# Inverse square roots of a two-layer graph network: from eight VectorE steps to one power on GpSimd

## The reference, cut to what matters

```python
x = _layernorm(x + _L0_gnn_ref(x, ...))   # attention over edges and self loops, then elu, residual, norm
x = _layernorm(x + _L1_gnn_ref(src, dst, x, edge_attr_3, ...))
...
# in _L0_gnn_ref
h = x + jax.nn.elu(proj)
out = (h - mu) * jax.lax.rsqrt(var + LN_EPS) * gamma + beta
...
# in _L1_gnn_ref
d = jax.nn.gelu(layer_norm(x @ Wd1 + bd1, g1, b1), approximate=False)
d = jax.nn.gelu(layer_norm(d @ Wd2 + bd2, g2, b2), approximate=False)
logits = w1[target] - w2[source] + d
out = jax.ops.segment_sum(a * (w3[source] + d), target, num_segments=m)   # a: softmax over a target's edges
```

## Time and profile before

| | us |
|---|---|
| runs, median of 3 | 2307.57 |
| runs, lowest and highest | 2290.02, 2311.89 |
| span of the profiled execution | 2281.3 |
| TensorE busy | 1697.7 (74%) |
| VectorE busy | 1608.6 (71%) |
| GpSimd busy | 1071.7 (47%) |
| ScalarE busy | 704.6 (31%) |

### The profile page before, as it was taken

One profiled execution on the slowest core, in us unless ns is written; L12 is line 12 of the kernel. 1 busy time (PEld: TensorE's weight loads), 2 busy tenths in 40 slices (PEclk: granted clock), 3 DMA queues, 4 the chain that ended last, 5 costly groups with the idle time before them and its releaser, 6 DMA issues. The chain is left out here.

```text
span 2281.3 us, 29583 instructions
## 1 busy us (share of the span) xinstructions
PE 1697.7 (74%) x6749; PEld 925.5 (41%) x6749; DVE 1608.6 (71%) x4249; ACT 704.6 (31%) x1168; POOL 1071.7 (47%) x1254
## 2 busy tenths in 40 slices
PE   6888798888878880099999999358676766667673
PEld 4555565555555540023333333247433333333331
DVE  2667676676767678657666766448598887878786
ACT  2545454454555440012222222025311111111111
POOL 3555554455555440002434444610267676667764
PEclk9999898999999985579778988668799888889886
DMA  2333333343334341101111111100112111112120
GB/s 69 102 110 123 108 120 109 103 125 108 120 113 126 107 115 35 27 11 25 37 33 36 39 35 31 35 5 3 30 43 47 42 46 41 46 44 50 43 49 14
DMA packets 154993, 142.83 MB, mean 63 GB/s; under 512 B 83688, under 2 KB 103103, under 8 KB 154948
## 3 DMA queue, kind: packets, MB, share of 16 engines
q1 hardware_dynamic: 122948, 112.22, 16.2%
q0 software_dynamic: 32000, 30.10, 6.7%
HBM read 71.30 MB, written 73.65 MB: 64 GB/s over the span
## 5 line engine op out<-in xcount | busy, mean ns | idle before, releaser
L415 POOL DMA_INDIRECT dense_pairs<-in_x_dram,dense_stage x400 | 411.1, 1028 | 128.1 <-issue 127.8
L1011 PE MATMUL bank<-first_zb,Mstack 128*64 128x512 f32 x400 | 246.0, 713 | 2.7 <-DVE first_zb L1091 2.2
L1452 POOL DMA_INDIRECT out_dram<-second_orow,second_stage x200 | 199.5, 997 | 85.1 <-issue 62.0
L1444 POOL DMA_INDIRECT second_pairs<-x_table,second_stage x200 | 209.3, 1047 | 61.6 <-issue 55.3
L967 POOL DMA_INDIRECT x_table<-first_xr,first_stage x200 | 198.2, 991 | 61.4 <-issue 60.7
L1091 DVE TENSOR_TENSOR first_zb<-bank,XT 128x512 f32<-128x512 f32 x200 | 135.2, 688 | 88.3 <-PE bank L1004 57.7
L961 POOL COPY first_stage<-first_rows 128x4 int32 (+1 forms) x50 | 10.1, 203 | 384.5 <-DVE first_xr L1160 259.5
L450 PE MATMUL bank<-dense_xT,Mblk 128*128 128x512 f32 x196 | 117.4, 684 | 63.2 <-ACT dense_xT L520 60.2
L455 PE MATMUL bank<-dense_hb,prm 128*128 128x512 f32 x196 | 128.4, 742 | 47.5 <-DVE dense_hb L580 43.2
L477 PEld LDWEIGHTS bank<-prm,dense_xT 128*128 128x128 f32 x784 | 122.1, 222 | 59.8 <-issue 59.8
L585 DVE TENSOR_SCALAR dense_v<-bank 128x8 f32<-128x8 f32 x98 | 16.0, 163 | 166.5 <-remote 132.7
(11 more groups left out here) (267 smaller groups left out, 3885.7 us busy)
## 6 DMA issues: line engine op xcount, KB each, us to landing
dense_rows<-in_x_dram SPq DMA_DIRECT2D x98, 256.0 KB
x_table<-dense_xr SPq DMA_DIRECT2D x98, 256.0 KB
out_dram<-dense_orow SPq DMA_DIRECT2D x98, 256.0 KB
dense_pairs<-in_x_dram,dense_stage POOLq DMA_INDIRECT x400
target_rows<-first_xr SPq DMA_DIRECT2D x50, 128.0 KB
second_pairs<-target_rows SPq DMA_DIRECT2D x50, 128.0 KB
second_mask<-mask_rows SPq DMA_DIRECT2D x50, 128.0 KB
first_mask<-mask_rows SPq DMA_DIRECT2D x50, 64.0 KB
```

Of the source, the lines that this page charges most:

```text
L415: pool.indirect_dma_start(out=pairs[a][:, j % 4, F * (j // 4):F * (j // 4) + F], out_offset=None, in_=x, in_offset=bass.IndirectOffsetOnAx ...
L1011: nc.tensor.matmul(pY[64 * s:64 * s + 64, :], Mstack[:, h, :], zb[(n - 2) % 4][:, :], start=(h == 0), stop=(h == H - 1)).then_inc(z_used, 1)
L1444: pool.indirect_dma_start(out=pairs[u.off % 2][:, j, 0:F], out_offset=None, in_=x1, in_offset=bass.IndirectOffsetOnAxis(ap=stage[a][:, j:j ...
L1452: pool.indirect_dma_start(out=out, out_offset=bass.IndirectOffsetOnAxis(ap=stage[a][:, 4 + j:5 + j], axis=0), in_=orow[a][:, j, :], in_off ...
```

## The change

Two small constant tiles are set up, `half` (-0.5) and `epsilons`. `root_step` and everything that fed it is gone. POOL takes each root as `tensor_tensor(..., half, ALU.pow)`, with the addition of eps before it on POOL too, but for the inner norm's of the node and first stages, which stays on VectorE (`keep_variance`). The two outer roots of the node stage, which before had v+eps and v(1+eps)+eps squared, now have s+eps and s+eps^2/(1+eps), and the factor (1+eps)^-0.5 moves into `orow`. In the node stage the eight gathers of an edge unit are spread: four in each slot, two before and two after `second_roots`. In the first stage the scatters are split around the roots. In the distance stage POOL has a program of its own. In the second stage `roots(u-3)` stands between the gather of u and the scatter of u-5.

```diff
-MAGIC = float(0x5F1FFFF9)
-def root_step(nc, dve, k, v, w, ta, tb, step, before, made):
...
-ROOT_STEPS = 8
+EPS_OUT = EPS * EPS / (1.0 + EPS)
+OUT_SCALE = (1.0 + EPS) ** -0.5
...
+                nc.vector.memset(half[:, :], -0.5)
+                nc.vector.memset(epsilons[:, 0, :], EPS)
+                nc.vector.memset(epsilons[:, 1, :], EPS_OUT)
...
-                def edge_unit(e):
-                    atleast(pool, pair_turned, e.count(-1))
-                    pool.wait_ge(sources_staged, e.count(1))
-                    stage_targets(e)
-                    gather(e, range(4))
-                    pool.wait_ge(targets_staged, e.count(1))
-                    stage_sources(e.next())
-                    gather(e, range(4, 8))
+                def first_roots(u):
+                    pool.wait_ge(v1_made, u.count(1))
+                    atleast(pool, scaled, u.count(0))
+                    nc.gpsimd.tensor_tensor(w1[:, :], v[:, :], half[:, 0:8], ALU.pow).then_inc(r1_made, 1)
+                def second_roots(u):
+                    b = u.off % 2
+                    pool.wait_ge(y_summed, u.count(1))
+                    atleast(pool, r2_made, u.count(0))
+                    nc.gpsimd.tensor_tensor(v2[:, :].rearrange("p (a r) -> p a r", a=2), epsilons[:, :, :],
+                                            s2[b][:, :].unsqueeze(1).to_broadcast([128, 2, 8]), ALU.add).then_inc(v2_made, 1)
+                    pool.wait_ge(v2_made, u.count(1))
+                    atleast(pool, out_made, u.count(-3))
+                    nc.gpsimd.tensor_tensor(w2[u.off % 4][:, :], v2[:, :], half[:, :], ALU.pow).then_inc(r2_made, 1)
                 def slot(u):
                     if u.static() and u.count(0) == 0:
                         stage_sources(EdgeUnit(0, 0))
+                    if u.back(2).valid(DENSE):
+                        first_roots(u.back(2))
                     if u.off % 2 == 1 and u.edge(0).valid(UNITS):
-                        edge_unit(u.edge(0))
+                        e = u.edge(0)
+                        atleast(pool, pair_turned, e.count(-1))
+                        pool.wait_ge(sources_staged, e.count(1))
+                        stage_targets(e)
+                        gather(e, range(2))
+                    if u.off % 2 == 0 and u.edge(1).next().valid(UNITS) and not (u.static() and u.count(0) == 0):
+                        e = u.edge(0)
+                        pool.wait_ge(targets_staged, e.count(1))
+                        stage_sources(e.next())
+                        gather(e, range(4, 6))
+                    if u.back(3).valid(DENSE):
+                        second_roots(u.back(3))
+                    if u.off % 2 == 1 and u.edge(0).valid(UNITS):
+                        gather(u.edge(0), range(2, 4))
+                    if u.off % 2 == 0 and u.edge(1).next().valid(UNITS) and not (u.static() and u.count(0) == 0):
+                        gather(u.edge(0), range(6, 8))
                 slots(pool, DENSE, 6, slot)
...
-                def add_eps(u):
+                def keep_variance(u):
                     dve.wait_ge(var_made, u.count(1))
-                    atleast(dve, roots_made, u.count(0))
-                    nc.vector.tensor_scalar(v[:, 0:8], pR[:, 0:8], EPS, None, ALU.add).then_inc(v1_made, 1)
-                def root(u, k):
-                    if k == 1:
-                        if u.valid(DENSE):
-                            dve.wait_ge(v1_made, u.count(1))
-                        atleast(dve, v2_made, u.count(-1))
-                    if k == ROOT_STEPS:
-                        atleast(dve, out_made, u.count(-2) if u.valid(DENSE) else min(u.count(-2), DENSE))
-                        atleast(dve, scaled, u.count(0) if u.valid(DENSE) else DENSE)
-                    root_step(nc, dve, k, v[:, :], w[:, :], ta[:, :], tb[:, :], root_steps, u.count(0), roots_made)
+                    atleast(dve, r1_made, u.count(0))
+                    nc.vector.tensor_scalar(v[:, :], pR[:, 0:8], EPS, None, ALU.add).then_inc(v1_made, 1)
                 def scale(u):
                     b = u.off % 2
-                    dve.wait_ge(roots_made, u.count(1))
+                    dve.wait_ge(r1_made, u.count(1))
                     dve.wait_ge(g_rows_made, u.count(1))
                     atleast(dve, y_made, u.count(0))
...
-                def keep_sums(u):
-                    dve.wait_ge(y_summed, u.count(1))
-                    dve.wait_ge(roots_made, u.count(2))
-                    nc.vector.tensor_scalar(v[:, 8:16], s2[:, :], EPS, None, ALU.add)
-                    nc.vector.tensor_scalar(v[:, 16:24], s2[:, :], 1.0 + EPS, EPS * EPS, ALU.mult, ALU.add)\
-                        .then_inc(v2_made, 1)
+                    atleast(dve, v2_made, u.count(-1))
+                    nc.vector.tensor_reduce(s2[b][:, :], q2[b][:, :, :], AX.X, ALU.add).then_inc(y_summed, 1)
                 def finish_x1(u):
                     b = u.off % 2
-                    dve.wait_ge(roots_made, u.count(3))
+                    dve.wait_ge(r2_made, u.count(1))
                     atleast(dve, stored[b], u.halves(0) * 32)
                     nc.vector.tensor_tensor(xr[b][:, :, :], yc[u.off % 4][:, :, :],
-                                            w[:, 8:16].unsqueeze(2).to_broadcast([128, 8, F]), ALU.mult)
+                                            w2[u.off % 4][:, 0:8].unsqueeze(2).to_broadcast([128, 8, F]), ALU.mult)
                 def finish_out(u):
-                    nc.vector.tensor_tensor(orow[u.off % 2][:, :, :], yc[u.off % 4][:, :, :],
-                                            w[:, 16:24].unsqueeze(2).to_broadcast([128, 8, F]), ALU.mult)\
-                        .then_inc(out_made, 1)
+                    nc.vector.scalar_tensor_tensor(orow[u.off % 2][:, :, :], yc[u.off % 4][:, :, :], OUT_SCALE,
+                                                   w2[u.off % 4][:, 8:16].unsqueeze(2).to_broadcast([128, 8, F]),
+                                                   ALU.mult, ALU.mult).then_inc(out_made, 1)
...
+                def first_roots(u):
+                    pool.wait_ge(v1_made, u.count(1))
+                    atleast(pool, scaled, u.count(0))
+                    nc.gpsimd.tensor_tensor(w1[:, :], v[:, :], half[:, 0:8], ALU.pow).then_inc(r1_made, 1)
+                def second_roots(u):
+                    pool.wait_ge(s_made, u.count(1))
+                    atleast(pool, r2_made, u.count(0))
+                    nc.gpsimd.tensor_tensor(v2[:, :], s2[:, :], epsilons[:, 0, :], ALU.add).then_inc(v2_made, 1)
+                    pool.wait_ge(v2_made, u.count(1))
+                    atleast(pool, flagged, u.count(0))
+                    nc.gpsimd.tensor_tensor(w2[:, :], v2[:, :], half[:, 0:8], ALU.pow).then_inc(r2_made, 1)
                 def slot(u):
                     if u.static() and u.count(0) == 0:
                         stage_part(u, 0, a_staged)
-                    u = u.back(4)
-                    if not u.valid(PAIRS):
-                        return
-                    pool.wait_ge(xr_made, u.count(1))
-                    pool.wait_ge(a_staged, u.count(1))
-                    stage_part(u, 1, b_staged)
-                    scatter(u, 0)
-                    pool.wait_ge(b_staged, u.count(1))
-                    stage_part(u.back(-1), 0, a_staged)
-                    scatter(u, 1)
+                    o = u.back(4)
+                    if o.valid(PAIRS):
+                        pool.wait_ge(xr_made, o.count(1))
+                        pool.wait_ge(a_staged, o.count(1))
+                        stage_part(o, 1, b_staged)
+                        scatter(o, 0, range(2))
+                    if u.back(3).valid(PAIRS):
+                        second_roots(u.back(3))
+                    if o.valid(PAIRS):
+                        scatter(o, 0, range(2, 4))
+                    if u.back(2).valid(PAIRS):
+                        first_roots(u.back(2))
+                    if o.valid(PAIRS):
+                        pool.wait_ge(b_staged, o.count(1))
+                        stage_part(o.back(-1), 0, a_staged)
+                        scatter(o, 1, range(4))
...
+                    def roots(n, u):
+                        pool.wait_ge(smd[n], u.count(1))
+                        nc.gpsimd.tensor_tensor(v[n][:, :], s2[n][:, :], epsilons[:, 0, :], ALU.add).then_inc(vmd[n], 1)
+                        pool.wait_ge(vmd[n], u.count(1))
+                        atleast(pool, nmd[n], u.count(0))
+                        nc.gpsimd.tensor_tensor(w[n][:, :], v[n][:, :], half[:, 0:8], ALU.pow).then_inc(rmd[n], 1)
+                    def slot(u):
+                        if u.valid(PAIRS):
+                            roots(0, u)
+                        if u.back(2).valid(PAIRS):
+                            roots(1, u.back(2))
+                    slots(pool, PAIRS, 3, slot)
...
+                    def roots(u):
```

(16 more changed lines are left out.)

162 lines of the change are left out of this document (39 added, 123 removed).

## The result

| | before | changed |
|---|---|---|
| median of 4 runs, us | 2302.17 | 2929.37 |
| lowest and highest | 2290.02, 2311.89 | 2922.17, 2933.79 |
| span of the profiled execution | 2281.3 | 2929.9 |

The ratio is 1.2745, 95% interval [1.2672, 1.2817]: 627 us slower, where 330 were forecast, with 2850 as the upper end of the range. The direction was right, the size half of it. Where the runs of a kernel fall into a faster and a slower group, a ratio compares the faster ones, so it can differ a little from the ratio of two medians.

A forecast was written before the change was run, and what follows sets the result against it. TensorE was busiest in the node and first stages, level with VectorE in distance; VectorE in the second. 190 + 115 - 15 + 40 = +330 on the 2281.3 us span gives 2611; with the median's 26 above it, 2638; range 2370 to 2850.

The forecast's parts named there:

- the power: POOL's inverse root, all four stages: taken as 0.45 us for 4 columns, 0.6 for 8, 0.9 for 16; at most 1.65.
- rival (a): All stages: the power is slow, some 3 us whatever the width; about 3370 us, chance 8%.
- Node stage: POOL's work for a slot is 8.2 us, as long as the slot; 8.7 us a slot taken, +40 us.
- The spread gathers' gain: Node stage: shorter gather bursts can shorten VectorE's late wait for the variance, 132.7 us in total before.
- Second stage: POOL's roots close a loop, so it can't run ahead: 16.6 us a unit against 12.5, +190 us.
- the loop: Second stage: hold, sum, addition and power, scatters, gathers, landing, turn, next hold; 16.2 us in all.
- the 0.4 that I had added for late wake-ups: Second stage: allowance on the round of 16.2 us, making 16.6, for wake-ups that come late.
- First stage: Roots between POOL's scatters make `yb` start 5.6 us later; 5.4 us for about 21 pairs, +115 us.
- Distance stage: Loop of sum, two roots in a row on POOL and one norm: 3.9 us against 4.45, -15 us.
- (b): Rival, node and second stages: POOL and VectorE hold each other up, or late wake-ups do; about 2800 us, chance 16%.
- (c): Rival, faster: the loops don't bite, since the sums reach POOL before it comes to them; 2080 us, chance 6%.

The follow-up runs named there:

- e4: Changed kernel with a multiplication by -0.5 in place of every power: 2401 us, 534 less than the changed kernel on the same chip.
- e11: Kernel before with only the node stage changed, its power of second_roots on 8 columns in place of 16: 2420 us beside 2343.
- e10: Kernel before with only the node stage's gathers spread, each four behind a wait for the variance, roots on VectorE: 2192 us beside 2343, ratio 0.935.
- e9: e8 with the copy of the scan's last column back right behind its scan: 2319 us beside 2343 for the kernel before, ratio 0.989.
- e12: Kernel before with only the distance stage changed, both sums of squares moved ahead of the two norms: 2421 us beside 2343, ratio 1.032.
- e13: e10 once more on a further chip: 2170 us beside 2300 for the kernel before, ratio 0.941.
- e14: e8 once more, on the chip of e15: 2297 us beside 2300 for the kernel before, ratio 1.003.
- e15: e9 once more, on the chip of e14: 2289 us beside 2300 for the kernel before, ratio 1.005.
- e7: e3 with VectorE's sum of squares moved ahead of the hold: 2061 and 2103 us in two runs beside 1987 for the kernel before.
- e3: Kernel before with only the second edge stage changed: 2274 us, +290.
- e2: Kernel before with only the first edge stage changed: 2191 us, +206.
- e8: e2 with both of POOL's roots moved ahead of its wait for xr: 2030 us beside 1987 for the kernel before, ratio 1.022.

## Why the prediction was wrong

**The mis-sized term is the power.** "I take 0.45 us for 4 columns, 0.6 for 8 and 0.9 for 16, nearer to the copy, since it is one instruction" was the choice that failed, and "above by the eight steps that it replaces, 1.65 us" was a bound that was none for 16 columns. The time grows with the columns, and the number of instructions in the program says nothing of that. I took one upper bound for every width, and rival (a) had 3 us whatever the width. That rival was right for the 16 columns alone.

**Node stage**, +40 forecast, +226 measured. POOL's sum of a slot with the measured prices is 8.2 + 2.2 + 1.1 + 0.15 = 11.6, against 10.6. The sum had 2.2 us of gaps and hops in it, where POOL sat idle for 1.2 a slot (1020 - 908 us, over 95.5 slots). I had written that POOL's work was "as long as the slot", so each microsecond more would count in full. e4 and e11 show that it does: the power's width sets the slot. The spread gathers' gain that I counted on is there (e10 against e9 and e12, e13 against e14 and e15, each on its chip: 1.3 to 1.7 us a slot), and the changed kernel shows no late wake-up at all, but a slot that POOL's queue sets at 10.6 us has no use for it.

**Second stage**, +190 forecast, +203 measured. The mechanism was right in every step, and e7 shows that it is mostly the loop that costs and not the power. The power was 0.6 us too little, and the 0.4 that I had added for late wake-ups was not needed: no row of this trace names "remote", and 16.2 + 0.6 is the 16.8 of the round shown.

**First stage**, +115 forecast, +184 measured. `yb` starts 7.1 us later than before, where 5.6 were forecast, two powers of 1.68 for 0.6. Pairs are 28.1 us apart (281 VectorE instructions in 395 us, 20 a pair), 9.3 more. What is left of that, some 2 us, fits TensorE, which is busy 20.8 us a pair (292 in 395) in place of 17.6 for the same matmuls, at 0.68 of its clock in place of 0.85. No run tests this part. A change of the granted clock was not in the sum.

**Distance stage**, -15 forecast, +15 measured: 0.64 + 2 x 2.0 + 0.64 = 5.3 with the measured 1.64, against 5.19. With the power's price as the trace has it, the formula gives what was measured, and with a multiplication in its place (e4) the stage is faster than before.

**Rivals.** (a) was wrong in mechanism for 4 and 8 columns and in its total (3370). (b) is there, and small. VectorE is not held: `orow` starts 0.32 us into the power of 508.57 and takes 0.70, as `hb` and `xr` do. POOL's instructions are a little longer: `second_roots` runs beside these three, each with two inputs from SBUF, and there the addition takes 0.22 to 0.77 us and the power 2.93 to 3.50 (0.31 and 3.20 at 508, 0.23 and 2.94 at 519), while `first_roots`, mostly beside none of them, takes 1.67. Means against shortest durations, that is some 0.3 us a slot, 30 of the 226 us. In the prediction's the VectorE step has one input, so those rows show a step that took longer and not a pair of two-input instructions. (c) fell: the loops bite, as the queues' order said.

The sum redone with the three measured prices, and all else as forecast (node slot 11.6 or, with POOL's idle time as it was, 10.6): +225 to +320, +160, +23, +215, so 2930 to 3030. The forecast's structure stands; the one price without a row is what was missing. That the low end hits 2929 has some luck in it: it takes POOL's idle time from the result, and the first stage has 24 us less than measured.

## What to carry to other kernels

Before work is moved to an idle engine, price its operation there at the real width. Where no row has it, don't take the cheap end for the likeliest (the power cost 2.3 to 3.4 times what I took), and every term that hangs on it moves together. A queue that runs ahead of the others is worth more than its idle share says: one instruction that waits for the present unit closes a loop through everything behind it, and its place in the order, not its duration, is then the price (e3 against e7, e2 against e8). Try the parts of a change alone: here one of them, the spread with its wait, was a gain of 6% by itself and lost in a change that cost 27%.
